# Injected rows of the first 14 chunks in an array of their own, and how far GpSimd leads the loop of a two-layer graph network

## What is computed

```python
# layer 0; each node has one of 2 types, each edge one of 3
h1, h2, h3, h4 = (node_proj(x, W, b, node_type) for W, b in ...)   # [3125, 64] each
w5e = edge_feat @ W5[edge_type] + b5[edge_type]                     # [100000, 64]
num = sum(h3[edge_dst] * (h4[edge_src] + w5e), axis=-1)
score = softmax((num / sqrt(16))[:, None], axis=-1)[:, 0]
msg = score[:, None] * (h2[edge_src] + w5e)
x = layernorm(x + h1 + segment_sum(msg, edge_dst))
# layer 1: a softmax over each node's incoming edges, then
# x = layernorm(x + (x + agg) @ Wm + bm)
```

## Time and profile before

| | before |
|---|---|
| three runs | 2247.61, 2242.93, 2236.8 us |
| median | 2242.93 us |
| the profiled execution | 2247.74 us |
| its span in the trace | 2245.8 us |
| mean granted TensorE clock | 0.886 of full speed |
| busy: TensorE / its weight loads | 1747.1 us (78%) / 1108.5 us (49%) |
| busy: VectorE | 1602.6 us (71%) |
| busy: GpSimd | 1294.3 us (58%) |
| busy: ScalarE | 757.1 us (34%) |

### The profile page before, as it was taken

One profiled execution on the slowest core, in us unless ns is written; L12 is line 12 of the kernel. 1 busy time (PEld: TensorE's weight loads), 2 busy tenths in 40 slices (PEclk: granted clock), 3 DMA queues, 4 the chain that ended last, 5 costly groups with the idle time before them and its releaser, 6 DMA issues.

```text
span 2245.8 us, 29209 instructions
## 1 busy us (share of the span) xinstructions
PE 1747.1 (78%) x9112; PEld 1108.5 (49%) x9112; DVE 1602.6 (71%) x3058; ACT 757.1 (34%) x1397; POOL 1294.3 (58%) x1348
## 2 busy tenths in 40 slices
PE   6453889898889889888873487888878787878873
PEld 5222556665666556555662144454445444544442
DVE  7422677777777777677768377788778786878786
ACT  3100222222222222222222144455455545455461
POOL 6365555555666565565633666666666665656624
PEclk9876999999999999999986688899999998989885
DMA  8942444545554555454443145555545555545442
GB/s 274 369 96 83 131 137 134 156 134 154 138 150 141 144 145 144 137 146 133 139 133 93 39 117 148 148 161 153 148 147 150 150 148 143 152 144 151 144 151 57
DMA packets 220072, 323.65 MB, mean 144 GB/s; under 512 B 62802, under 2 KB 127948, under 8 KB 219789
## 3 DMA queue, kind: packets, MB, share of 16 engines
q1 hardware_dynamic: 132958, 150.94, 22.9%
q0 software_dynamic: 43056, 68.05, 13.7%
q10 hardware_dynamic: 43904, 102.79, 12.6%
HBM read 188.35 MB, written 133.22 MB: 143 GB/s over the span
## 4 chain that ended last, share of the span: by engine, by line
PE 28%; issue 17%; another core or an unknown queue 16%; ACT 12%; DVE 12%; ACTq 3%; POOL 2%; DMA 1%; DVEq 0%; SPq 0%; POOLq 0%
PE wide L957 8%; PE wide L1069 5%; ACT block L860 3%; PE wide L931 3%; PE wide L966 2%; ACTq L853 2%; ACT prob_wide L837 2%; PE wide L923 2%; ACT msg L838 2%; ACT block L841 1%; DVE h3d L1363 1%; PE bank L1005 1%; ACT block L830 1%; DVE featm L1354 1%
## 5 line engine op out<-in xcount | busy, mean ns | idle before, releaser
L672 POOL DMA_INDIRECT rows<-d_x,idx x588 | 559.7, 952 | 350.2 <-issue 155.3
L662 POOL DMA_INDIRECT block<-d_h,idx x482 | 462.9, 960 | 302.9 <-issue 126.8
L1069 PE MATMUL wide<-late,ntype_i 125*128 125x512 bf16 x975 | 240.4, 404 | 54.7 <-DVE ntype_i L1492 49.5
L662 POOL DMA_INDIRECT rows<-d_h,idx x160 | 153.8, 961 | 151.6 <-PE wide L931 58.3
L1363 DVE TENSOR_TENSOR_SCAN h3d<-keep,h3d,bank 128x512 f32<-128x512 bf16 x98 | 124.9, 1275 | 159.1 <-issue 114.4
L1069 PE MATMUL wide<-edge_lists,ntype_i 125*128 125x512 bf16 x936 | 229.2, 401 | 11.9 <-issue 11.5
L931 PE MATMUL wide<-typed,zeros 128*128 128x128 f32 (+1 forms) x1364 | 185.0, 283 | 13.1 <-issue 13.1
L1080 PE MATMUL wide<-ident,block 128*128 128x128 f32 x784 | 134.4, 320 | 72.0 <-ACT block L860 43.9
L1069 PEld LDWEIGHTS wide<-late,ntype_i 125*128 125x128 bf16 x975 | 101.1, 104 | 176.2 <-DVE ntype_i L1492 49.9
L957 PE MATMUL wide<-late,ntype_i 125*128 125x512 bf16 x702 | 177.1, 409 | 12.5 <-issue 5.0
L957 PE MATMUL wide<-edge_lists,ntype_i 125*128 125x512 bf16 (+1 forms) x702 | 170.7, 396 | 11.6 <-issue 9.2
(11 more groups left out here) (255 smaller groups left out, 3214.2 us busy)
## 6 DMA issues: line engine op xcount, KB each, us to landing
d_run<-block ACTq DMA_DIRECT2D x98, 512.0 KB
d_inj<-zeros SPq DMA_DIRECT2D x28, 896.0 KB
inj<-d_inj SPq DMA_DIRECT2D x98, 256.0 KB
d_run<-stage ACTq DMA_DIRECT2D x98, 256.0 KB
feat<-in_ea16x3T SPq DMA_DIRECT2D x196, 96.0 KB
types<-d_type SPq DMA_DIRECT2D x196, 64.0 KB
keep<-d_keep SPq DMA_DIRECT2D x196, 64.0 KB
keep<-d_pen SPq DMA_DIRECT2D x196, 64.0 KB
```

Of the source, the lines that this page charges most:

```text
L662: pool.indirect_dma_start(out=ring[c % RING][:, j, h, :], out_offset=None, in_=d_h24, in_offset=bass.IndirectOffsetOnAxis(ap=idx[:, c, at: ...
L672: pool.indirect_dma_start(out=rows1[c % RING1][:, j, h, :], out_offset=None, in_=d_x1, in_offset=bass.IndirectOffsetOnAxis(ap=idx[:, c, at ...
L1069: ins = pe.matmul(p_hot[s], table[q][:, SPLIT * k:SPLIT * (k + 1), :].rearrange("p b c -> p (b c)"), hot[s][:, k, :], start=(k == 0 and q ...
```

## The change

**An array of its own.** `d_early` holds the injected rows of the first 14 chunks (`EARLY`): 14336 rows in four zero units (`EARLY_UNITS`). VectorE makes a second list, `early_i`, with four more small operations behind `first_i`; nodes whose first edge lies in a later chunk point to spare rows. GpSimd scatters all 25 tiles to `d_early` ahead of its first gather, and to `d_inj` behind `gather0(10)` (`SCATTER_BEHIND`), where it waits for `d_inj`'s zeros. `load_inj` reads `d_early` for chunks 0 to 13, and at chunk 14 waits for both scatters. The fix goes to `d_early`.

**Zeros.** SyncE clears the four units of `d_early` and three of `d_inj` at first, seven of `d_inj` between the stores of `d_h24`, and the last 14 in the loop, two behind the loads of each of chunks 2 to 8. The first four units of `d_inj`, whose rows nobody reads, are not cleared. A unit is written as 512 rows of 1792 bytes from a quarter of the zero tile, where it was 128 rows of 7168.

**Index work.** The two subtractions and the clearing of the table's spare rows leave VectorE's row search and index work: `left0` stands behind `early_i`, `table[2]` behind the last index.

**GpSimd's lead.** `gather0(0)` and `gather0(1)` wait until TensorE has looked up and encoded unit 0 or 1 (`looked`), `gather0(2)` until unit 1 is picked. GpSimd then leads the loop by 4 chunks up to chunk 7, by 6 up to chunk 23, and by 8 from there, where it led by 8 throughout.

**TensorE's lead.** `PICK_LEAD` is 2 in place of 4 and `FIRST_STEP` 0 in place of 3, so that units 2 and 3 are picked in the loop and pieces stand in steps 0 to 93.

```diff
-AHEAD = 6
 ZEROS = 28
-ZEROS_EARLY = 7
+ZEROS_EARLY = 3
+ZEROS_LATE = 14
+EARLY = 14
+AHEADS = ((24, RING), (RING, RING - 2), (0, RING - 4))
+EARLY_UNITS = 4
+EARLY_ROWS = EARLY * 2 * CH
+SCATTER_BEHIND = 10
...
-PICK_LEAD = 4
+PICK_LEAD = 2
...
-FIRST_STEP = 3
+FIRST_STEP = 0
...
+        def rows_ahead(c):
+
+            return next(ahead for first, ahead in AHEADS if c >= first)
+
+        encoded_by = {c: 2 * c + 2 for c in range(PICK_LEAD)}
...
+            no_rows = zeros[:, 0:7 * C].unsqueeze(1).to_broadcast([P, 4, 7 * C])
+
+            def clear(first, behind):
+                for z in range(first, behind):
+                    sp.dma_start(flat[z], no_rows).then_inc(s_injzero, 16)
...
-            for z in range(ZEROS_EARLY):
-                sp.dma_start(flat[z], zeros[:, :]).then_inc(s_injzero, 16)
+            for z in range(EARLY_UNITS):
+                sp.dma_start(flat_early[z], no_rows).then_inc(s_early, 16)
+            clear(EARLY_UNITS, EARLY_UNITS + ZEROS_EARLY)
...
-            for first, behind, zeroed, zeros_to in ((0, 10, ZEROS_EARLY, 11), (10, 20, 11, 14), (20, NT, 14, ZEROS)):
+            for first, behind, zeroed, zeros_to in ((0, 10, EARLY_UNITS + ZEROS_EARLY, 11), (10, 20, 11, ZEROS_LATE), (20, NT, ZEROS_LATE, ZEROS_LATE)):
...
+                if c == EARLY:
+                    sp.wait_ge(s_inj, 2 * 16 * NT)
+                sp.dma_start(inj[s][:, :, :], (d_early if c < EARLY else d_inj)[bass.ds(c * (2 * CH), 2 * CH), :]
...
-            sp.wait_ge(s_injzero, 16 * ZEROS)
...
+                clear(min(ZEROS_LATE + 2 * (c - 2), ZEROS), min(ZEROS_LATE + 2 * (c - 1), ZEROS))
...
-                if c in row_unit:
-                    pool.wait_ge(picked[0], row_unit[c] + 1)
-                if c >= RING:
-                    pool.wait_ge(q2_ready[c % 2], (c - RING) // 2 + 1)
+                if c in encoded_by:
+                    pool.wait_ge(looked, encoded_by[c])
+                if c == PICK_LEAD:
+                    pool.wait_ge(picked[0], PICK_LEAD)
+                ahead = rows_ahead(c)
+                if c >= ahead:
+                    pool.wait_ge(q2_ready[c % 2], (c - ahead) // 2 + 1)
...
+            pool.wait_ge(s_sel, KT)
+            pool.wait_ge(s_early, 16 * EARLY_UNITS)
+            pool.wait_ge(s_rows_i, 1)
+            scatter(d_early, early_i)
             pool.wait_ge(s_h24, 16 * 6)
-            for c in range(AHEAD):
+            for c in range(CHUNKS):
                 gather0(c)
...
+                if c == SCATTER_BEHIND:
+                    pool.wait_ge(s_injzero, 16 * (ZEROS - EARLY_UNITS))
+                    pool.wait_ge(s_inj, 16 * NT)
+                    scatter(d_inj, first_i)
...
-            act.wait_ge(s_injzero, 16 * ZEROS)
+            act.wait_ge(s_zeros, 1)
...
-                if i == BOUNDS[3]:
-                    for q in range(3):
-                        then(dve.memset(table[q][:, NT:, :], 0.0))
-                    dve.wait_ge(s_rounded, 1)
-                    dve.tensor_tensor(left0, x_sb[:, :, :], table[0][:, 0:NT, :], ALU.subtract).then_inc(s_left, 1)
...
+            then(dve.scalar_tensor_tensor(tmp_n[:, :], tmp_n[:, :], float(-EARLY_ROWS), node[:, :], ALU.add, ALU.subtract))
+            then(dve.tensor_tensor(tmp_n[:, :], tmp_n[:, :], in_row[:, :], ALU.mult))
+            then(dve.scalar_tensor_tensor(tmp_n[:, :], tmp_n[:, :], float(EARLY_ROWS), node[:, :], ALU.add, ALU.add))
+            dve.tensor_copy(early_i[0:NP, :], tmp_n[:, :]).then_inc(s_rows_i, 1)
+            dve.wait_ge(s_rounded, 1)
+            dve.tensor_tensor(left0, x_sb[:, :, :], table[0][:, 0:NT, :], ALU.subtract).then_inc(s_left, 1)
```

More of the change, by code:

```diff
@@ L494, in _ @@
                     sp.dma_start(of_node[a:b, first:behind, :], H[a:b, first:behind, C:3 * C]).then_inc(s_h24, 16)
[L495 to L496 removed]
+                clear(zeroed, zeros_to)
             def load_features0(s, r, of_edge):
@@ L1180, in _ @@
             then(dve.tensor_scalar(first_i[:, :], node_i[:, :], float(DUMP), None, ALU.add))
+            then(dve.tensor_scalar(early_i[:, :], node_i[:, :], float(EARLY_ROWS), None, ALU.add))
             dve.wait_ge(s_edges, 64)
@@ L1270, in _ @@
             dve.wait_ge(s_mbcol, 1)
-            dve.wait_ge(s_rounded, 2)
-            dve.tensor_tensor(table[2][:, 0:NT, :], left0, table[1][:, 0:NT, :], ALU.subtract).then_inc(s_left, 1)
+            for q in range(3):
+                then(dve.memset(table[q][:, NT:, :], 0.0))
             dve.wait_ge(s_shift, 1)
```

47 lines of the change are left out of this document (20 added, 27 removed).

## The result

The changed kernel takes 2286.92 us (median of 2281.24, 2286.92 and 2297.77) against 2242.93: a ratio of 1.0206, 95% interval 1.0134 to 1.0278. It is slower by 44 us, where 31 us less were forecast, and outside the range. Its profiled execution is the one of 2297.77 us, with a span of 2296.0, 50.2 us over that of before.

A forecast was written before the change was run, and what follows sets the result against it. TensorE was taken to bound the loop; in the head, a late list, GpSimd's scatter and late signals. 52.6 us gained, less 15 for catching up and 7 for end pieces, say 31: 2212 us from 2242.9, range 2178 to 2247.

The forecast's parts named there:

- The reading of the profile: Head of the kernel: the longer a burst of indirect DMAs has run, the later TensorE's signals arrive, up to 15.66 us.
- Item 1: Index work in the head: without VectorE's stops in the row search, early_i comes at 65.5 us, against first_i at 73.56.
- Item 2: Early scatter in the head: 25 tiles of 1.28 us, to 97.7 us; chunk 1's rows in SBUF by 118 us.
- Item 3: TensorE's shorter lead in the head: chunk 1's projection at 130 us, bounds 118 to 141, 75.6 us earlier than before.
- Item 4: Ten loop steps from chunk 1 to chunk 11: one more unit, 11.2 us a step, chunk 11 at 242 us.
- Item 5: Late scatter behind chunk 10's gathers: from 214 to 246 us, chunk 11's projection at 259, 52.6 us left of the gain.
- Item 6: GpSimd catching up from 214 us, issuing 60 to 80 us more without pause: costs nothing to 31 us, taken as 15.
- the rival in which GpSimd becomes the bound: Loop's first quarter, from chunk 7's step: signals held as long as the burst lasts; 2257 us, slower; chance 0.08.
- Item 7: End of layer 0's loop: steps 91 to 93 get one more piece each, costing 7 us.
- Item 8: Zeros in the loop, chunks 2 to 8: priced at nothing, DMA share 0.89; uncovered they would cost 34 us.

The follow-up runs named there:

- e4: The changed kernel with GpSimd leading by 4 chunks all through layer 0, instead of 4, then 6, then 8: ratio 0.9969 to the kernel before.

## Why the prediction was wrong

**The reading of the profile** held: late signals, tied to how long GpSimd issues. So did the head. Item 1: `early_i` at 65.4 (65.5 said). Item 2: the scatter ended at 103.5, not 97.7; issues of 1.77, 1.84, 4.38 and 1.63 us instead of 0.97 make up 5.7 us of that. The Trainium skill ("SBUF — State Buffer", section "SBUF: two separate sides") has VectorE lock GpSimd out there; the trace agrees with long issues beside VectorE's work, and it cost no more than the sentence said. Item 3: chunk 1 at 138.0, within 118 to 141, but 8 us behind the 130 taken: one look-up was answered only behind the run.

**Item 4** took 11.2 us a step. Steps 5 and 6 took 23.5 and 21.2, since the lead grows from 4 to 6 at chunk 8, which lets chunks 7 to 10 go in one run of 26 (179.3 to 211.5). I had read `AHEADS` as pure cover and priced no run for either growth: these two steps took 22 us more than the item has, and with the 8 us of item 3, chunk 9 came at 243.9 for 219.6. The second, at chunk 24, is most of the 25.0 us from chunk 11 to 24 (chunk 20 is 24.9 us behind chunk 19). e4 has neither.

**Item 5** set the late scatter at 214 us; it came at 241.6, as the last zeros follow the delayed step 6. In e4, without the first run, it is 219.6: the working was right and its input, item 4, was not.

**Item 6 is the step that failed.** It took 15 us, at most 31, for a run of 60 to 80 us, by signals 13 us late in steps of 17 us. The run of 64 us held TensorE almost throughout: 50.3 us from chunk 9 to 10, where 11.2 were taken, and 28.3 to chunk 11. That one step costs 39 us. I had rows for it: the scan at 202.87 came only behind the end of a run of 63 us. Read as a delay of a signal it is 15.66 us; read as "until the run ends" it is the rest of the run. I gave that reading 0.08, as the rival in which GpSimd becomes the bound, because of one signal answered at 145.23, and because I took GpSimd's own waits to end a run. They can't while it is behind. The rival's price, 2257 us, was too small also, by the growth of the lead. In sum: chunk 11 came at 322.6 for 259, 63.6 us late; from there to chunk 90 35.2 us were lost for 15; the end cost 0.7 for 7, and 3.2 came behind it. That is the distance of 81 us between 31 less and the trace's 50 more.

**Item 7** took 7 us for three pieces: chunks 90 to 97 take 59.1 us for 58.4. **Item 8** held: with a DMA share of 0.80 and 0.64, TensorE's and VectorE's waits for DMAs from chunk 1 to 9 sum to 1.7 us.

**What stays open.** Why TensorE's matmuls come 2.1 or 2.8 us apart at such a rate of issues: the runs show under which rate it happens, not by which part of the chip. Every timed execution here was also recorded, so no run shows whether the hold is there without recording. The Trainium skill ("NOTIFIC — the notification-queue block", section "7.1 Overflow: three behaviours, one of which stalls the engine") says that the block's internal pipeline holds producers back rather than lose a record; no run here can show whether that is at work. The cause of the 10.2 us between chunks 24 and 90 was not found; 9.5 of them lie behind chunk 40. e4 takes 691.5 us there and before 695.1, with the same pieces as the changed kernel's 705.3.

## What to carry to other kernels

Before moving work ahead of a loop, count how many indirect DMAs GpSimd will then issue in a row and when it is behind: in this kernel 0.70 or more of them per us for more than some 10 to 15 us hold TensorE up, and a longer lead, or one that grows on the way, makes just such runs. If an engine stands with "issue" as its only reason while another works without a pause, put a pause into the other as the first experiment; where the pauses end, a hold that begins right there settles it. And price a wait of which few cases are seen by both readings, as so much delay and as "until the other has done", before choosing.
